# A fused attention and feed-forward kernel: q and k summed and split inside their PSUM bank by TensorE and ScalarE, with a new order of the steps

## What is computed

```
x = x + attention_a(layernorm(x))        # 16 heads of 8, rotary embedding, causal over 256 tokens
x = x + ffn(layernorm(x))                # fp4 block quantisation of x, of h and of the weights, inner size 352
x = x + attention_b(layernorm(x))        # groups of 32 tokens, rmsnorm of q and k, causal inside a group
x = x + ffn(layernorm(x))                # the same weights as the first ffn

q = q * cos + rotate_every_two(q) * sin  # in attention_a, and k likewise
```

## Time and profile before

| | before |
|---|---|
| runs | 606.18, 606.99, 609.55 us; median 606.99 us |
| the profiled execution | 605.69 us |
| its span, first to last instruction | 603.9 us (1.8 us of the time lie around it) |
| granted TensorE clock, mean | 0.815 of full speed |
| PE busy | 421.6 us |
| DVE, ACT, POOL busy | 364.0, 203.7, 179.8 us |

### The profile page before, as it was taken

The page is one execution under the profiler, slowest core; times in us unless marked ns, Lnnn a source line. Parts: engine busy times, 40 slices in busy tenths (PEclk is TensorE's granted clock), DMA queues, the critical chain, the costliest instruction groups (busy, mean ns, idle before and its releaser), DMA issues.

```text
span 603.9 us, 10380 instructions
## 1 busy us (share of the span) xinstructions
PE 421.6 (70%) x4061; PEld 268.8 (45%) x4061; DVE 364.0 (60%) x894; ACT 203.7 (34%) x548; POOL 179.8 (30%) x207
## 2 busy tenths in 40 slices
PE   0034577776866897889779687978878764968743
PEld 0023345454544564556555454554644342534422
DVE  3983418377585487757885769488585455062532
ACT  1010240522612642364366126524543313313310
POOL 9540200332332240442162306132324043020202
PEclk9985887778995898699989877999895858575865
DMA  7003130401451340117023303604003101300000
GB/s 233 3 26 80 46 62 2 109 0 30 80 105 34 77 105 3 30 39 149 12 80 74 63 10 107 107 5 110 6 4 92 22 3 47 68 2 10 1 9 9
DMA packets 59938, 31.04 MB, mean 51 GB/s; under 512 B 3249, under 2 KB 59505, under 8 KB 59889
## 3 DMA queue, kind: packets, MB, share of 16 engines
q1 hardware_dynamic: 59888, 30.37, 22.2%
HBM read 16.14 MB, written 13.63 MB: 49 GB/s over the span
## 4 chain that ended last, share of the span: by engine, by line
PE 54%; DVE 17%; ACT 10%; DMA 7%; POOL 5%; SPq 4%; issue 3%; POOLq 0%; DVEq 0%; ACTq 0%
PE bank L888 8%; PE bank L903 6%; PE bank L764 4%; PE bank L725 4%; PE bank L849 4%; PE bank L844 3%; PE bank L779 3%; DVE bmax L1251 3%; PE bank L693 3%; DMA Qf<-nmTf 3%; PE bank L857 2%; PE bank L896 2%; PE bank L768 2%; ACT probl L1005 2%; ACT prob L962 2%
## 5 line engine op out<-in xcount | busy, mean ns | idle before, releaser
L1251 DVE TENSOR_REDUCE bmax<-bank 128x3 f32<-128x384 f32 x128 | 63.2, 549 | 14.4 <-PE bank L749 13.7
L962 ACT ACTIVATE prob<-bank 128x384 f32<-128x384 f32 x128 | 56.4, 492 | 31.1 <-PE bank L768 30.4
L764 PE MATMUL bank<-Qf,Kf 128*128 128x256 bf16 x128 | 30.7, 330 | 30.4 <-DMA Qf<-nmTf 22.1
L1005 ACT ACTIVATE probl<-bank 128x512 f32<-128x512 f32 x64 | 38.2, 597 | 40.5 <-PE bank L849 40.0
L1332 DVE TENSOR_TENSOR xall<-bank,xall 128x128 f32<-128x128 f32 x32 | 9.3, 291 | 52.4 <-PE bank L903 52.2
L1077 POOL TENSOR_TENSOR qk<-ra,rb 128x512 f32<-128x512 f32 x8 | 11.9, 1484 | 86.8 <-DVE rb L1243 86.8
L1102 POOL TENSOR_TENSOR fb__w<-fb__w,fb__c 128x704 f32<-128x704 f32 x8 | 13.4, 1672 | 77.4 <-DVE fb__w L1213 77.4
L844 PE MATMUL bank<-maskb,identb 128*128 128x512 bf16 x64 | 28.7, 448 | 10.3 <-ACT probl L1005 7.0
L1323 DVE SCALAR_TENSOR_TENSOR fb__hg<-fb__th,bank 128x352 f32<-128x352 f32 x16 | 8.3, 518 | 43.3 <-ACT fb__th L1023 43.2
L779 PE MATMUL bank<-prob,Vf 128*32 128x128 f32 (+1 forms) x512 | 28.8, 344 | 4.3 <-ACT oTf L923 4.3
L888 PE MATMUL bank<-wguT,fb__xqT 128*128 128x352 f32 x64 | 28.1, 569 | 5.3 <-DVE fb__h L1324 3.3
(11 more groups left out here) (212 smaller groups left out, 1055.6 us busy)
## 6 DMA issues: line engine op xcount, KB each, us to landing
scr_f<-partsf SPq DMA_DIRECT2D x16, 192.0 KB, 2.4
Qf<-scr_f SPq DMA_DIRECT2D x16, 192.0 KB
Kf<-scr_f SPq DMA_DIRECT2D x16, 192.0 KB
scr_l<-partsl SPq DMA_DIRECT2D x16, 192.0 KB, 2.4
Ql<-scr_l SPq DMA_DIRECT2D x16, 192.0 KB, 3.9
Kl<-scr_l SPq DMA_DIRECT2D x16, 192.0 KB, 4.9
scr_f<-partsf SPq DMA_DIRECT2D x16, 128.0 KB, 1.9
scr_l<-partsl SPq DMA_DIRECT2D x16, 128.0 KB, 1.9
```

The costliest lines, as they stand in the source:

```text
L764: pe.matmul(ring(2 * g + j)[:, 0:256], Kf[:, g, 0:128], Qf[:, 2 * g + j, 0:256], start=True, stop=True)
L962: act.activation(prob[:, h % 8, :], bank[h % 3][:, 0:384], ACT.Exp).then_inc(f.s_exp, 1)
L1005: act.activation(probl[:, u % 2, :, :].rearrange("p c n -> p (c n)"), bank[4][:, :], ACT.Exp).then_inc(l.s_exp, 1)
L1251: dve.tensor_reduce(bmax[:, h, :], bank[h % 4][:, 0:384].rearrange("p (n k) -> p n k", k=P), AX.X, ALU.max).then_inc(bmax_done, 1)
```

## The change

The sum and the two subtractions of each split become matmuls that accumulate in the PSUM bank. DVE writes the cos product back into bank 0. PE adds `rb` to it with a float32 identity matmul of 512 columns. ACT copies the bank to the first bf16 part, PE takes that part off the bank with a bf16 matmul by minus identity (`negb`), ACT copies the rest, PE takes it off, ACT copies the third part. Attention_b does the same in bank 5 (ACT's `local1` changes as its `front1` below), without the sum. So the third part is made by ACT, not by POOL; the DMAs are as before. The second pass of `front2` starts its ring at bank 1 and waits for the third part of the next batch before its second pair of heads, when bank 0 comes in. All rows of `TIMES` and the list `FFN_TURNS` are new: turns of part a and part b are now interleaved (up, up, down, down).

```diff
@@ FFN_TURNS
-    ("a", 2, "up"), ("a", 2, "down"), ("a", 3, "up"), ("a", 3, "down"),
-    ("b", 0, "up"), ("b", 0, "down"), ("a", 4, "up"), ("a", 4, "down"),
-    ("b", 1, "up"), ("b", 1, "down"), ("a", 5, "up"), ("a", 5, "down"),
-    ("b", 2, "up"), ("b", 2, "down"), ("a", 6, "up"), ("a", 6, "down"),
-    ("b", 3, "up"), ("b", 3, "down"), ("a", 7, "up"), ("a", 7, "down"),
-    ("b", 4, "up"), ("b", 4, "down"), ("b", 5, "up"), ("b", 5, "down"),
+    ("a", 2, "up"), ("a", 2, "down"), ("b", 0, "up"), ("a", 3, "up"),
+    ("b", 0, "down"), ("a", 3, "down"), ("a", 4, "up"), ("b", 1, "up"),
+    ("a", 4, "down"), ("b", 1, "down"), ("b", 2, "up"), ("a", 5, "up"),
+    ("b", 2, "down"), ("a", 5, "down"), ("b", 3, "up"), ("a", 6, "up"),
+    ("b", 3, "down"), ("a", 6, "down"), ("b", 4, "up"), ("a", 7, "up"),
+    ("b", 4, "down"), ("a", 7, "down"), ("b", 5, "up"), ("b", 5, "down"),
     ("b", 6, "up"), ("b", 6, "down"), ("b", 7, "up"), ("b", 7, "down"),
@@ TIMES
...
     "pe.local1": """
...
+342 344 348 350 352
+398 399 402 404 405
+429 430 433 435 436""",
     "pe.local2": """
...
+381 385 407 408 410 412 414 416 417 419 421 423 425 426
+427 428 437 438 439 440 441 442 444 446 448 450 451 452
+453 454 455 456 458 460 461 463 464 465 466 467 468 469""",
     "pe.ffn_a2": """
...
+401 403 406 418 420 422 424""",
     "pe.ffn_b2": """
...
+431 432 434 443 445 447 449
+457 459 462 470 471 472 473
+474 475 476 477 478 479 480""",
@@ PE
             def ring(h):
-                return bank[h % 3]
+                return bank[(h + 1) % 3]
+
+            def take_off(b, a, held, parts):
+                for p in range(2):
+                    yield
+                    pe.wait_ge(a.s_part[p], b + 1)
+                    pe.matmul(held[:, :], negb[:, :], parts[:, p, :, :].rearrange("p a t -> p (a t)"), start=False, stop=True,
+                              skip_group_check=True).then_inc(a.s_rest, 1)
@@ PE front1
+                yield
+                pe.wait_ge(rope_mul, b + 1)
+                pe.matmul(bank[0][:, :], identf[:, :], flat(rb), start=False, stop=True, skip_group_check=True).then_inc(qk_summed, 1)
+                yield from take_off(b, f, bank[0], partsf)
@@ PE front2
+                        if g == 1 and b < NBATCH - 1:
+                            pe.wait_ge(f.s_part[2], b + 2)
@@ PE local1
-                turn(bank[5], qkn[:, :, :, :].rearrange("p a t d -> p (a t d)"), 2 * T).then_inc(l_qkT_ps, 1)
+                for n in range(2 * T):
+                    mm = pe.matmul(bank[5][:, n * P:(n + 1) * P], qkn[:, n // T, n % T, :], identf[:, :], start=(n == 0), stop=True, skip_group_check=True)
+                mm.then_inc(l_qkT_ps, 1)
+                yield from take_off(b, l, bank[5], partsl)
@@ PE local2
-                                pe.wait_ge(l.s_rest, b + 2)
+                                pe.wait_ge(l.s_part[2], b + 2)
@@ ACT
+            def split(b, a, held, parts, p):
+                copy(parts[:, p, :, :].rearrange("p a t -> p (a t)"), held[:, :]).then_inc(a.s_part[p], 1)
@@ ACT front1
-                act.wait_ge(qk_ready, b + 1)
-                copy(partsf[:, 0, :, :], qk[:, :, :]).then_inc(f.s_part[0], 1)
-                yield
-                act.wait_ge(f.s_rest, b + 1)
-                copy(partsf[:, 1, :, :], restf[:, :, :]).then_inc(f.s_part[1], 1)
+                act.wait_ge(qk_summed, b + 1)
+                split(b, f, bank[0], partsf, 0)
+                for p in range(1, 3):
+                    yield
+                    act.wait_ge(f.s_rest, 2 * b + p)
+                    split(b, f, bank[0], partsf, p)
@@ POOL front1
-                pool.wait_ge(rope_mul, b + 1)
-                pool.tensor_tensor(qk[:, :, :], ra[:, :, :], rb[:, :, :], ALU.add).then_inc(qk_ready, 1)
-                yield
-                pool.wait_ge(f.s_part[0], b + 1)
-                pool.tensor_tensor(restf[:, :, :], qk[:, :, :], partsf[:, 0, :, :], ALU.subtract).then_inc(f.s_rest, 1)
-                yield
-                pool.wait_ge(f.s_part[1], b + 1)
-                pool.tensor_tensor(partsf[:, 2, :, :], restf[:, :, :], partsf[:, 1, :, :], ALU.subtract).then_inc(f.s_part[2], 1)
-                yield
@@ POOL local1
-                pool.wait_ge(l.s_rest, b + 1)
-                pool.wait_ge(l.s_part[1], b + 1)
-                pool.tensor_tensor(partsl[:, 2, :, :], restl[:, :, :], partsl[:, 1, :, :], ALU.subtract).then_inc(l.s_part[2], 1)
-                yield
@@ DVE setup
+            dve.tensor_scalar(negb[:, :], identf[:, :], -1.0, None, ALU.mult)
@@ DVE front1
-                dve.tensor_tensor(flat(ra), bank[0][:, :], ropet[:, 0:2, :].rearrange("p a t -> p (a t)"), ALU.mult)
+                dve.tensor_tensor(bank[0][:, :], bank[0][:, :], ropet[:, 0:2, :].rearrange("p a t -> p (a t)"), ALU.mult)
@@ DVE local1
-                dve.wait_ge(l.s_part[0], b + 1)
-                dve.tensor_tensor(flat(restl), bank[5][:, :], partsl[:, 0, :, :].rearrange("p a t -> p (a t)"),
-                                  ALU.subtract).then_inc(l.s_rest, 1)
-                yield
```

More of the change, by code:

```diff
@@ L37 @@
 VW = 32
+VS = 16
 GROUPS = H // 4
@@ L60 @@
 6 7
[L61 to L65, removed]
+10 11
+17 18
+23 24
+30 31
+37 38""",
     "sp.front2": """
@@ L68 @@
 5
-8
-13
-19
[L72 to L86, removed]
+9
+16
+22
+29
+36
+43""",
+    "sp.local1": """
+8 12
+14 15
+20 21
+27 28
+34 35
+41 42
+46 47
+50 51""",
+    "sp.local2": """
+13
+19
 26
 32
-39
+40
 44
-48
-52""",
+49
+53""",
     "sp.store": """
@@ L95 @@
 33
[L96 to L99, removed]
+39
+45
+48
+52
 54
@@ new lines @@
+68 70 74 76 79
+110 113 118 121 124
+163 165 171 174 179
+222 225 228 230 233
+286 288 292 295 298""",
+    "act.front2": """
[7 rows of a table added]
+340 345 347 348 349 350 351 353 354 356 357 358 359 360 361 362 363 365 366 368 369 372""",
+    "act.local1": """
+65 66 67 69 71
+103 104 105 106 107
+155 157 159 160 161
+210 211 213 215 216
+264 266 270 271 273
+324 325 327 328 329
+375 376 379 381 382
+402 403 406 408 409""",
+    "act.local2": """
[7 rows of a table added]
+425 426 427 429 430 432 433 434 436 437 438 439 440 441""",
+    "act.ffn_a2": """
@@ L223 @@
+39 42 47 62 64
+72 75 80 95 100
+120 127 132 149 151
+166 170 178 206 207
+212 214 217 245 249
+282 285 291 309 316
+335 338 343 370 371
+378 380 383 396 399""",
+    "act.ffn_b2": """
+154 156 158 197 204
+220 224 240 261 265
+268 269 272 297 301
+321 322 326 352 364
+373 374 377 386 390
+404 405 407 418 422
+428 431 435 442 443
+444 445 446 447 448""",
+    "pool.front1": """
+0
+2
+3
+7
+14
+21
+30
+41""",
     "pool.front2": """
 1
[L225 to L229, removed]
-68
-81""",
-    "pool.local1": """
-23 26 29
@@ L234 @@
-36 37 41
-43 49 53
-54 58 66
-67 72 78
-80 85 86
-90 92 95
-101 102 104""",
-    "pool.ffn_a1": """
-11 14
-19 22
-30 34
-40 42
-56 57
-70 71
-83 84
-94 96""",
-    "pool.ffn_a2": """
-18
-28
-39
-45
-62
-77
-88
-98""",
-    "pool.ffn_b1": """
-46 48
-61 64
-76 79
-87 89
-91 97
-99 100
-106 107
-109 110""",
-    "pool.ffn_b2": """
-55
-69
-82
-93
-103
-105
-108
-111""",
+4
+9
+16
+24
+33
+45
+54""",
+    "pool.local1": """
+11 12
+17 19
+26 28
+35 37
+43 47
+55 57
+63 65
+69 72""",
+    "pool.ffn_a1": """
@@ L277 @@
+5 6
+10 13
+18 20
+27 29
+36 38
+48 49
+56 58
+64 66""",
+    "pool.ffn_a2": """
+8
+15
+22
+32
+40
+51
+60
+68""",
+    "pool.ffn_b1": """
+23 25
+34 39
+44 46
+52 53
+61 62
+70 71
+74 75
+77 78""",
+    "pool.ffn_b2": """
+31
+42
+50
+59
+67
+73
+76
+79""",
     "dve.weights": """
-0 2 3 4 5 6 7 8 10 11 13 15 16""",
+1 2 3 4 5 6 7 8 10 11 12 15 17""",
     "dve.front1": """
-1 9 12
-14 17 35
-36 37 59
-60 63 90
-91 98 127
-132 135 175
-186 189 228
-238 241 278""",
+0 9 13
+14 16 35
+36 37 60
@@ new lines @@
+347 350 356
+370 373 378""",
+    "dve.local2": """
+105 139 142
+145 190 192
+195 239 244
+247 285 288
+292 333 337
+339 368 371
+374 386 387
+389 398 399""",
+    "dve.ffn_a1": """
+40 57 59 61
+72 86 94 96
+112 130 132 134
+154 160 175 177
+202 205 207 209
+256 261 265 268
+304 306 308 310
+349 352 353 354""",
+    "dve.ffn_a2": """
+64 65 66 67 68 70 75
+100 101 102 103 104 106 107
+137 138 140 141 143 147 150
+183 186 187 188 189 197 199
+219 225 228 230 232 240 242
+280 284 286 287 289 297 298
@@ L351 @@
+328 331 332 334 335 345 346
+359 361 362 363 365 367 369""",
+    "dve.ffn_b1": """
+144 146 148 151
+193 198 218 224
+245 248 250 252
+291 294 295 296
+338 340 342 343
+372 375 376 377
+388 390 391 392
+400 401 403 405""",
+    "dve.ffn_b2": """
+161 178 179 182 185 191 194
+234 236 237 238 241 249 253
+257 275 278 281 283 290 293
+302 321 326 329 330 336 341
+351 355 357 358 360 364 366
+379 380 381 382 383 384 385
+393 394 395 396 397 402 404
+406 407 408 409 410 411 412""",
 }
@@ L396, in build @@
         identb = sb("identb", [P, P], BF16)
+        negb = sb("negb", [P, P], BF16)
         half = sb("half", [P, 4])
@@ L961, in front2 @@
                                 act.wait_ge(f.s_o_ps, b * GROUPS + h // 4 - 1)
```

(10 more changed lines are left out.)

185 lines of the change are left out of this document (48 added, 137 removed), and 66 rows, old and new, of the table TIMES.

## The result

The changed kernel takes 550.25 us (median of 4 runs, 546.66 to 554.10), against 606.59 us for the kernel before in the same runs: a ratio of 0.9068, 95% interval 0.8995 to 0.9140. The forecast was 596, its range 577 to 615. The direction was right, the size was not: 56 us came off where 12 were summed.

What follows compares the result with a forecast made beforehand. PE was taken as nearly full from 200 to 450 us, a chain of waits as deciding the tail. Terms summed to -11.8 from 605.69, giving 593.9; carried to the median 595.2, stated as 596, range 577 to 615.

Steps and rivals of the forecast that it cites:

- Start, -2.1: Split of batch 0, where nothing else runs: 5.6 us instead of 7.74, a gain of 2.1, between 1.4 and 3.
- The wait for Kf, -2.7: PE's 2.72 us wait for Kf of batch 6 at 335.42 goes: -2.7, between 0 and -2.7.
- +8 in front1: Bank 0 is free later, so the second pair of heads waits 1.2 us seven times: +8, between 0 and +25.
- +6 in local1: Two takings-off per batch on PE in attention_b, 6.1 to 9.3 us, plus later tail waits: +6, between 3 and 11.
- The tail, -11: From 493 on, three pairs of turns instead of four, one pair 8.0 plus 3 for hand-overs: -11, between -4 and -16.
- rival "no change": Tail gain and middle cost cancel, the last batch's chain keeping its length: 604 to 610 us, chance 0.13.
- The order before 493, -2: b4 and the first local stage of batch 6 move into a stretch that shortens little: -2, between +3 and -8.
- in the middle, -8: From 200 to 450 us, ups fill a fifth of PE's 43.6 idle us: -8, between 0 and -22.
- rival "much faster": Turns of banks 6 and 7 bound the middle too: -22 there, tail -16, perhaps a faster clock: 576 us, chance 0.20.
- DVE beside POOL, an estimate of 3 us left out: Less POOL work frees DVE's two-port operations: some 3 us, sum 591; left out as lying on DVE, not the chain.

Runs made afterwards that it cites:

- e1: New split with the order and turns of the kernel before, added steps put between their old neighbours: 613.91 us, ratio 1.0215 against the kernel before.
- e14: Kernel before with interleaved turns, the order of e2 improved by a long search over single moves of steps: 535.48 us, ratio 0.8847.
- e16: Kernel before, split and turns unchanged, only its order improved by a long search: 558.60 us, ratio 0.9219.
- e4: Kernel before with six matmuls that nobody reads in each of the eight waits for the maxima: 585.76 us, ratio 0.9774.
- e5: Kernel before, split and turns unchanged, only TIMES made anew by one placement method: 582.71 us, ratio 0.9684.
- e6: Kernel before with interleaved turns, TIMES made by the same method as e5: 564.99 us, ratio 0.9397.
- e2: Kernel before, old split, with the changed kernel's tables (TIMES and interleaved turns) and places for POOL's old steps: 593.05 us, ratio 0.9876.
- e7: Changed kernel with the turns of before, TIMES made by the same method as e5: 581.53 us, ratio 0.9639.
- e8: Changed kernel with its interleaved turns, TIMES made by the same method as e5: 573.37 us, ratio 0.9535.
- e15: Changed kernel with its order improved by the same search as e14: 556.69 us, ratio 0.9192.
- e9: Changed kernel with four unread POOL operations per batch added on their own tiles, 42.1 us of POOL work: 554.87 us, ratio 0.9218.
- e18: e14 with unread matmuls in PE's waits of the last batch and four more in each wait for the maxima: 536.17 us, ratio 0.8871.

## Why the prediction was off

**Start, -2.1: right, and a little small.** The third part of batch 0 ends at 42.57 (43.8 was said), and the first maxima of batch 0 start at 52.72 instead of 55.73, 3.0 us sooner. The split took 4.0 us of the 5.6 said (7.7 before): the sum 1.12 instead of 1.9, a taking-off 0.39 instead of 0.58, a hand-over some 0.05 instead of 0.15.

```profile
37.91 0.68 DVE L1252 TENSOR_TENSOR rb<-bank,ropet 128x512 f32<-128x512 f32 x1
38.65 1.12 PE L739 MATMUL bank<-rb,identf 128*128 128x512 f32 x2 [0.87 <-DVE rb L1252]
...
41.97 0.60 ACT L939 ACTIVATE partsf<-bank 128x512 bf16<-128x512 f32 x1 [0.48 <-PE bank L713]
```

**The wait for Kf, -2.7: right.** It is gone, in e1 too, so by the split; the only one left is that of batch 0. But PE's one wait for Kl of attention_b (L837, L821 before) grew from 2.4 us to 7.1 in e1 and 7.4 in the kernel after, which no term had.

**The split's price, +8 in front1 and +6 in local1: right in sum for the old order, not in its parts.** With the start's -2.1 and Kf's -2.7 that is +9.2; e1's ratio is +13 us, with an interval of 4 to 22. But the waits of the second pair for the third part, sized at seven of 1.2 us, are six in e1, 4.4 us in all; Kl's longer wait, and against it the higher clock in e1, were not in the sum. The durations were right: 384 and 415 ns for a taking-off against 383 taken. Not priced at all were the transposes of `local1`, of which the diff shows that they turn into products: +3.3 us of PE. In the order of after the waits for the third part nearly vanish, 1.1 us once where seven of a microsecond were foretold; that the order puts other work between is likely and was not tested.

**The tail, -11: too much, -4.2 measured.** There is one pair of turns less, as said. But from the end of part a of batch 7 the two last stages of attention_b decide, `local2` of batch 6 at 485.08 and of 7 at 514.39, and behind that stands one batch's own chain: 34.8 us to the end of the span, 33.3 before. That is the mechanism of the rival "no change", true for this stretch alone.

**The order before 493, -2, and in the middle, -8: the step that failed.** It said that PE is nearly full from 200 to 450, that most of its 43.6 idle us are short waits inside attention, which stay, and that the new order could fill at most half of them. It booked -10 where the measured gain up to the end of part a is 50.5, of which the start and Kf are 5 or 6. Of the 50.5, PE's idle time gives 38.9 (142.7 to 103.7) and its busy time 11.5 (350.7 to 339.1), with nearly as many matmuls issued. Three things were wrong in it.

First, the waits did not stay. The idle time ahead of 200 us fell by 7.4 us only; from there to the end of part a it fell from 55.6 to 24.1, more than half. The waits for the maxima, which it counted as cover for the new matmuls alone, went from 22.1 to 4.0. In e1 the split's own matmuls bring them to 10.1, and in e14 and e16 an order alone to 2.6 and 5.2. Work of other stages can stand in them: attention_b of batch 0 ends at 208.2 in the trace after, 36.6 us sooner than at 244.8, so there is more to choose from, earlier. Before, then after:

```profile
244.44 0.41 DVE L1303 TENSOR_TENSOR xall<-bank,xall 128x256 f32<-128x256 f32 x1
```
```profile
207.81 0.42 DVE L1308 TENSOR_TENSOR xall<-bank,xall 128x256 f32<-128x256 f32 x1
```

How much of the filling is owed to that earlier start was not tested.

Second, it took PE's busy time as given. At a clock of 0.91, a fuller PE is also a faster one: the group of L764 went from 330 to 286 ns, and PE's busy time fell by 16.8 us over the span although the new split adds 24.8 (21.5, and 3.3 for the transposes). e4 shows that this is cause and not company, as 2% came from filling alone, all of it busy time. The rival "much faster" had this for the tail only. The Trainium skill (TensorE: Matmul & The Clock Gate, "What's actually happening") has it that activity releases the throttle; e4 agrees, with 0.80 to 0.90 between 60 and 200 us.

Third, it asked what the turns allow and not what the ranks themselves cost. e16 against the kernel before is 47 us with ranks alone; the interleaved turns are worth 18 (e5 to e6) to 23 (e16 to e14) with the old split, which is near what the rival of 576 us gave the middle (-22), by luck: its reason, banks 6 and 7 handed over at once all along, is not what the trace has, where the eleven hand-overs from 200 us to 494 take 0.15 to 2.9 us.

So the order is what the gain needs: the split without it costs (e1), and orders without the split reach 559 and 535 us. How the 56 us of this very change divide between its ranks and its turns stays open, since its tables with the old split gave only 1% (e2) and its turns in series were not run with ranks as good. In no pair of runs with orders made in the same way (e5 and e7, e6 and e8, e14 and e15) is the new split, which gives the change its name, ahead by more than the intervals.

**DVE beside POOL, an estimate of 3 us left out: too small, but rightly left out.** The four groups of that DVE operation take 19.2 us in the kernel after and 30.5 before: 11.3 less. By e9 the effect is real on DVE. By the Trainium skill (SBUF — State Buffer, section "SBUF: two separate sides") a DVE operation in a two-port mode and one of POOL shut each other out for a whole instruction, and 343 against 1094 ns agrees. On the time of the kernel it is some 2% at most, and e9 can't tell it from nothing.

## What to carry to other kernels

Before a change of order is priced, do not take PE's idle time in a full-looking stretch as fixed: list its waits, and ask for each which step of another stage could stand in it. An order written by hand can hold back work that has been ready for long, and 8% lay in these tables without a single operation changed. Split a gain into busy and idle time of the fullest engine up to a fixed point of the work; here both fell, and that shows the clock's part. An edit that comes with a new order is to be run in both orders, each made for its code; the edit may bring nothing. And where a tuned order leaves TensorE short waits at a granted clock below 1, a few unread matmuls in them are a cheap test of what the clock is worth, as long as they fit the waits.

## What was not expected of the hardware

Seven waits of 3.2 us on average (the longest 3.6) went with a lowered clock in the whole middle: 48 matmuls put at the eight places took the granted clock from 0.80 to 0.90 and from 0.91 to 0.97 in two long stretches, and 2% off the time. Filling can also pay with one hand and take with the other: in the last pair of turns of e18 it raised the clock from 0.50 to 0.92 and shortened the chain by 4.0 us, and its own overrun took 2.7 back.
